# Row maxima of attention turned on VectorE instead of TensorE, and carried by four DMAs instead of two

## The chip, the cores and the metric

One core of one Trainium2 chip. The time is the device time of one execution in microseconds (us); lower is better.

## The reference

The input x has 8 batches of 1,024 tokens with 512 features. A layer of causal self-attention (16 heads of 32) with a residual and a layernorm is followed by a mixture-of-depths block: of each batch's 1,024 tokens, the 512 with the best router score go through a feed-forward net, and their result is added to the rows they came from.

```python
qkv = encodings @ W_attn + b_attn
scores = jnp.einsum('bhki,bhqi->bhkq', k, q) / math.sqrt(HEAD)
scores = jnp.where(mask, scores, jnp.float32(-10000.0))
attn = jax.nn.softmax(scores, axis=2)
combined = jnp.einsum('bhkq,bhkl->bhql', attn, v)
...
x = _layernorm(x + attn_out)
scores = jnp.einsum('bsd,d->bs', x, w_router)
top_scores, top_idx = jax.lax.top_k(scores, k)      # k = half of the tokens
h = gelu(selected @ W1 + b1);  processed = h @ W2 + b2
x = _layernorm(x + scatter(sigmoid(top_scores) * processed))
```

## The kernel before, in words

All five engines run hand-ordered streams that meet only through semaphores. A class `Table` lays the attention stage out in **beats**. A **unit** u (64 of them, `U = 8 * B`) is one batch, one group of four heads and one half of the queries (512). Two units, an even one (first half of the queries) and an odd one (second half), make a pair, and a pair takes 32 beats. Each engine's program walks over the beats n and issues in each what the table puts there, so the position in the table is only an order within each engine, not a time.

Per unit there are two passes over the scores. **Pass A** forms the scores with queries on the partitions, piece by piece (`a_piece` on TensorE, 11 pieces for an even unit, 27 for an odd one), into a ring of three PSUM banks (`A_BANKS`). VectorE takes the negated row maximum of each piece (`max_piece`) and collects them in `nm`: 128 queries by 16 numbers (4 heads by 4 blocks of 128 queries). **Pass B** (`b_tile`) forms the scores again with keys on the partitions. Its matmul has 98 rows in place of 96: rows 96 and 97 of `Qp` hold the negated maximum as a high and a low part, and the same rows of `Kp` hold ones, so that the maximum is subtracted inside the matmul. ScalarE then only takes the exponential (line 943). GpSimd masks and adds up (lines 795 and 818), and TensorE multiplies with V (line 1456) and forms the sums.

Pass A of an even unit lies at beats 0 to 8.5 of its pair, that of the odd unit at 8.5 to 30 (`A_AT`). Pass B lies at 28 to 36.5 and 36.5 to 58 (`B_AT`), so it runs into the next pair.

Between the two passes the 128 x 16 maxima must be turned to 16 x 128. In the kernel before this is an entry "F" of the ring at beat 15.99 or 31.99 (`F_AT`): `transpose_maxima` is one TensorE transpose (line 1411) into a ring bank. `shift_out` on VectorE copies it to `shs` as the high part (line 1061) and subtracts for the low part (line 1063). SyncE's queue then sends one DMA of 16 rows by 512 bytes for each part to rows 96 and 97 of `Qp` (line 670). The first B tile of the unit waits for both.

SyncE issues nearly every DMA of the kernel in the order of the table: loads of x and of the split weights, the stores and reloads of the attention output (`o_s`, `Ot`), and the packs of Q and K (`Qp<-nat`, `Kp<-nat`, line 687, three DMAs each). The attention stage also carries the "dense" work (projections, output projection O with its residual and layernorm statistics, sums N), cut into pieces and spread over the beats. After attention comes the feed-forward stage (lines 1491 and 1512), matmuls back to back.

Of the kernel before, what the change touches and what calls it, by code (L numbers as in the profile page):

```python
# [5 lines left out]
F32 = mybir.dt.float32  # L6
# [7 lines left out]
P = 128  # L14
# [19 lines left out]
BEATS = 16  # L34
A_AT = ((0.0, 8.5), (8.5, 30.0))
B_AT = ((28.0, 36.5), (36.5, 58.0))
F_AT = (15.99, 31.99)
A_BANKS = (0, 1, 2)
B_BANKS = (3, 4)
LAST_B = (4, 3, 0)  # L40
# [134 lines left out]
class Table:  # L175
# [68 lines left out]

    def streams(self):

        self.tiles, self.formed, self.products = {}, {}, {}
        ring = []
        for u in range(U):
            at, end = A_AT[u % 2]  # L250
            some = chunks(u)
            work = [1.3 if len(x[0]) == 4 else 0.8 if x[3] == 384 else 1.0 for x in some]
            for j, x in enumerate(some):
                p = u // 2 * 2 * BEATS + at + (end - at) * sum(work[:j]) / sum(work)
                ring.append((p, ("A", u, j, x)))
            ring.append((u // 2 * 2 * BEATS + F_AT[u % 2], ("F", u)))
            at, end = B_AT[u % 2]
            some = [(k, hh) for k in range(ksteps(u)) for hh in tiles_of(u, k)]
            work = [168 + 0.87 * width(u, k) * len(hh) for k, hh in some]
            for t, (k, hh) in enumerate(some):  # L260
                p = u // 2 * 2 * BEATS + at + (end - at) * sum(work[:t]) / sum(work)
                self.tiles.setdefault(int(p), []).append((p, (u, k, hh)))
                self.formed[u, k] = int(p + (end - at) * work[t] / sum(work) * (1 - 1 / len(hh)))
            for k in range(ksteps(u)):
                j, k1 = [(j, max(g)) for j, g in enumerate(PRODUCTS[u % 2]) if k in g][0]
                n = self.formed[u, k1] + PV_LAG[u % 2][j]
                assert not by_products(u) or n < self.beat["N", u]
                self.products.setdefault(n, []).append((u, k))
        self.scored = {}
        for b in range(B):  # L270
            self.scored[b] = self.beat["O", b, TT - 1] + 9 if b < B - 2 else self.beat["S", b]
            if b < B - 2:
                ring.append((self.scored[b] + 0.9, ("S", b)))
        self.ring, self.ring_no = {}, {}
        for j, (p, x) in enumerate(sorted(ring, key=lambda y: y[0])):
            self.ring.setdefault(int(p), []).append((p, j, x))
            self.ring_no[x[:3]] = j
# [85 lines left out]
def layer(nc, s, args, dr, cs, out):  # L363
    T = Table()
    x, xt, wqkv, wo, bat, b_out, w_router, W1, b1, W2, b2 = args
    with ExitStack() as st:
# [79 lines left out]
        maskA = sb("maskA", [P, 512], BF16)  # L446
        one32 = ones[:, 0:HD].bitcast(F32)
        nm = sb("nm", [P, 2, 2, HG, 4], F32)
        shs = sb("shs", [16, 2, P], F32R)
        lst_, lmv, lrs, lnb = sb("lnst", [P, 2, 6], F32), sb("lnmv", [P, 2, 2], F32), sb("lnrs", [P, 2, 2], F32), sb(  # L450
            "lnnb", [P, 2, 2], F32)
        li = sb("li", [P, 2, 4, 2], U32)
# [128 lines left out]
        def sync(e):  # L581
# [49 lines left out]
            for n in range(T.first, T.last):  # L631
# [29 lines left out]
                if n - 7 in load_v and 2 <= load_v[n - 7] < V_NEW:  # L661
                    q = load_v[n - 7]
                    e.wait_ge(s["v_split"], q + 1)
                    store(4 + q % 2, Wvf, s["v_st"])
                for a, x_ in T.ring_in(n - 1):
                    if x_[0] == "F":
                        u = x_[1]
                        e.wait_ge(s["a_max"], a + 1)
                        for j in range(2):
                            e.dma_start(Qp[96 + j:97 + j, u % 4, :, :].rearrange("a h (t n) -> a (h t) n", n=P)  # L670
                                        .bitcast(F32), shs[:, j, :].bitcast(F32)).then_inc(s["shift"], 16)
                for job in T.packs.get(n, ()):
                    e.wait_ge(*freed(job))
                    if job[0] == "Q":
# [351 lines left out]
        def vector(e):  # L1026
# [8 lines left out]

            def max_piece(j, u, i, piece):
                hh, qt, k0, w, part = piece
                if i == 0 and u >= 2:
                    e.wait_ge(s["a_mm"], T.ring_no["F", u - 2] + 1)
                e.wait_ge(s["a_mm"], j + 1)  # L1040
                if k0 < 512 * (u % 2):
                    ins = e.tensor_reduce(out=nm[:, u % 2, 0, hh[0], qt:qt + 1], in_=PS[:, A_BANKS[j % 3], :], op=ALU.max,  # L1042
# [9 lines left out]
                                                     accum_out=nm[:, u % 2, u % 2, h_, qt:qt + 1])  # L1052
                ins.then_inc(s["a_max"], 1)

            def shift_out(j, u):

                src = PS[0:16, A_BANKS[j % 3], 0:P]
                e.wait_ge(s["a_mm"], j + 1)
                if u:
                    e.wait_ge(s["shift"], 32 * u)  # L1060
                link(e.tensor_copy(shs[:, 0, :], src))
                linked()
                e.tensor_tensor(shs[:, 1, :], src, shs[:, 0, :].bitcast(F32), ALU.subtract).then_inc(s["a_max"], 1)

            def scores_out(j, b):
                e.wait_ge(s["a_mm"], j + 1)
# [2 lines left out]
                e.tensor_copy(sct[:, :], PS[0:TT, A_BANKS[j % 3], 0:P]).then_inc(s["a_max"], 1)  # L1069

            def ring_entry(j, x_):
                if x_[0] == "F":
                    shift_out(j, x_[1])
                elif x_[0] == "S":
                    scores_out(j, x_[1])
                else:
                    max_piece(j, *x_[1:])
# [149 lines left out]
            for n in range(T.first, T.last):  # L1227
# [9 lines left out]
                    ring_entry(*x_)  # L1237
                for job in todo:
                    evacuate(job)
                for x_ in some[1:]:  # L1240
                    ring_entry(*x_)
                for j in o_conv.get(n - 1, ()):
                    o = o_number(j)
                    t = j[2]
                    e.wait_ge(s["os_hi"], o + 1)
                    e.tensor_tensor(Os[:, 1, :, :], Ot[:, :, :], Os[:, 0, :, :].bitcast(F32),
                                    ALU.subtract).then_inc(s["os"], 1)
# [13 lines left out]
                if n in rank_beat:  # L1261
                    t = rank_beat[n]
                    if t == 0:
                        e.wait_ge(s["srow"], 16)
                    if t < TT:
                        count_ranks(e, s, cs, sc[:, 0, :], srow0, cmpb0, t)
                    else:
                        list_ranks(e, s, cs, 0)
                for k in range(KT):
                    if n - 6 - k in load_x:  # L1270
                        split_x(*load_x[n - 6 - k], k)
# [25 lines left out]
        def tensor(e):  # L1297
# [107 lines left out]
                                   start=True, stop=True)  # L1405
                ins.then_inc(s["a_mm"], 1)

            def transpose_maxima(j, u):
                e.wait_ge(s["a_max"], T.ring_no["A", u, len(chunks(u)) - 1] + 1)
                e.wait_ge(s["a_max"], j - 2)  # L1410
                e.transpose(PS[0:16, A_BANKS[j % 3], 0:P], nm[:, u % 2, u % 2, :, :].rearrange("p h t -> p (h t)"),
                            cs["identf"][:]).then_inc(s["a_mm"], 1)

            def transpose_scores(j, b):
                e.wait_ge(s["score"], TT * (b + 1))
                e.wait_ge(s["a_max"], j - 2)
                e.transpose(PS[0:TT, A_BANKS[j % 3], 0:P], sc[:, b, :], cs["identf"][:]).then_inc(s["a_mm"], 1)

            def ring_entry(j, x_):
                if x_[0] == "F":  # L1420
                    transpose_maxima(j, x_[1])
                elif x_[0] == "S":
                    transpose_scores(j, x_[1])
                else:
                    a_piece(j, *x_[1:])
# [1 line left out]
            def b_tile(u, k, hh):  # L1427
# [1 line left out]
                j = tiles_before(u, k) + tiles_of(u, k).index(hh)  # L1429
                w = width(u, k)  # L1430
                if k == 0 and hh[0] == 0:
                    e.wait_ge(s["shift"], 32 * (u + 1))
                if j == tiles_before(U - 1) + 2:
                    e.wait_ge(s["a_max"], len(T.ring_no))
                elif j >= 2:
# [123 lines left out]
        with nc.Block() as block:  # L1559
# [6 lines left out]

SEMAPHORES = ("c0", "bias", "b_scaled", "wq_in", "w1_in", "x0_hi", "rk0", "w_in", "w_hi", "w_split", "w_st", "v_in", "v_hi", "v_split", "v_st", "wo_in",
              "wo_hi", "wo_lo", "x_hi", "x_lo", "ones", "rows", "d_mm", "ev_v", "ev_a", "kq_hi", "a_mm", "a_max",
              "shift", "b_mm", "b_exp", "keep", "padd", "pv", "o_cp", "nln", "rinv", "ot", "os_hi", "os",
              "lmva", "rs", "hset", "oset", "score", "sge", "sig", "scd", "srow", "srow7", "rank_list", "v_link", "v_rank", "p_link",  # L1570
              "wlo2", "whi2", "fc", "f0", "f1", "f3", "fmv", "fst", "frs", "f_link", "p_sum", "ht", "t_hi", "hthi", "htlo", "up", "gelu",
              "ghi", "glo", "dn")
# [59 lines left out]
```

## Time and profile before

| what | value |
|---|---|
| time, median of 3 runs | 2560.07 us (2559.65 to 2562.88) |
| profiled execution: span from first to last instruction | 2558.8 us |
| TensorE busy | 2481.7 us, 97% of the span |
| VectorE / ScalarE / GpSimd busy | 65% / 47% / 61% |
| mean granted TensorE clock | 0.981 |

The page gives no device time of its own for the profiled execution; the median of the runs is 1.3 us above its span. Busy time of TensorE is modelled from pipelined matmuls: a matmul's duration is longer than the distance from its start to the next one's start, so the distance between starts is what it costs.

### The profile page before, as it was taken

How to read it: one execution, taken by the hardware profiler on the slowest of the kernel's cores; microseconds unless marked ns; L12 is line 12 of the kernel's file. 1: busy time of each engine (PE TensorE's matmuls, PEld its weight loads, DVE VectorE, ACT ScalarE, POOL GpSimd, SP SyncE). 2: the span in 40 equal slices, each digit the busy share in tenths (PEclk: the TensorE clock that was granted, in tenths of full speed). 3: DMA queues.
4: the chain of work that ended last, by engine and by line, in shares of the span. 5: the costliest groups of instructions: out<-in, count | busy, mean ns of one | idle time of the engine just before them, and what ended most of it. 6: DMA issues, size and time to landing. Idle time of an engine off the chain costs nothing.

```text
span 2558.8 us, 40698 instructions
## 1 busy us (share of the span) xinstructions
PE 2481.7 (97%) x14168; PEld 1834.9 (72%) x14168; DVE 1665.5 (65%) x4231; ACT 1190.7 (47%) x2034; POOL 1556.9 (61%) x1635
## 2 busy tenths in 40 slices
PE   7999999999999999999999999997999999999998
PEld 5666676777776777777776767773688888888886
DVE  6667677777776867877677777777555545553533
ACT  2555566656655655656656556565531111111110
POOL 1677788778887878888778877877232113121211
PEclk8999999999999999999999999998999999999999
DMA  7666677776577866767766676763420101010000
GB/s 146 90 108 139 126 144 172 140 150 157 129 144 130 193 128 127 175 127 153 151 145 146 125 167 137 155 154 97 152 91 25 34 25 42 25 34 25 22 29 17
DMA packets 167262, 286.46 MB, mean 112 GB/s; under 512 B 23121, under 2 KB 58001, under 8 KB 165906
## 3 DMA queue, kind: packets, MB, share of 16 engines
q1 hardware_dynamic: 159890, 267.01, 49.1%
q0 software_dynamic: 7168, 16.85, 2.1%
q8 instruction: 114, 1.87, 0.4%
q14 instruction: 90, 0.74, 0.1%
HBM read 116.97 MB, written 65.11 MB: 71 GB/s over the span
## 4 chain that ended last, share of the span: by engine, by line
PE 81%; POOL 2%; ACT 2%; DVE 1%; issue 1%; DMA 1%; SPq 1%; POOLq 0%; ACTq 0%; DVEq 0%
PE PS L1512 13%; PE PS L1491 13%; PE PS L1352 11%; PE PS L1438 10%; PE PS L1404 9%; PE PS L1456 8%; PE PS L1366 7%; PE PS L1360 6%; PE PS L1375 2%; POOL Pa L818 1%; PE PS L1368 1%; PE PS L1472 0%; PE PS L1333 0%; DMA h_s<-hs 0%; ACT Pm L943 0%
## 5 line engine op out<-in xcount | busy, mean ns | idle before, releaser
L818 POOL TENSOR_TENSOR Pa<-Pa,Pm 128x512 f32<-128x512 f32 (+1 forms) x602 | 743.8, 1259 | 114.4 <-ACT Pm L943 101.5
L1438 PE MATMUL PS<-Qp,Kp 98*128 98x512 f32 (+3 forms) x1536 | 494.9, 358 | 24.1 <-ACT Pm L943 13.2
L1404 PE MATMUL PS<-Kp,Qp 96*128 96x512 f32 (+3 forms) x1536 | 495.0, 359 | 17.4 <-DVE nm L1042 5.7
L943 ACT ACTIVATE Pm<-PS 128x512 f32<-128x512 f32 (+1 forms) x643 | 358.1, 568 | 282.6 <-PE PS L1438 243.5
L1042 DVE TENSOR_REDUCE nm<-PS 128x1 f32<-128x512 f32 x512 | 344.9, 687 | 183.7 <-PE PS L1404 183.6
L818 POOL TENSOR_TENSOR Pa<-Pa,P 128x512 f32<-128x512 f32 (+1 forms) x297 | 369.6, 1268 | 57.1 <-ACT P L943 50.1
L1404 PEld LDWEIGHTS PS<-Kp,Qp 96*128 96x128 f32 x1536 | 282.9, 193 | 118.5 <-issue 44.3
L1438 PEld LDWEIGHTS PS<-Qp,Kp 98*128 98x128 f32 x1536 | 281.7, 192 | 104.1 <-ACT Pm L943 27.4
L1050 DVE CUSTOM_DVE_ANT_0 PS<-PS,maskA 128x384 f32<-128x384 f32 (+3 forms) x512 | 245.9, 509 | 153.3 <-PE PS L1404 152.2
L908 ACT ACTIVATE G<-PS,b1c 128x512 f32<-128x512 f32 x128 | 88.2, 689 | 539.6 <-PE PS L1491 539.5
L1050 DVE CUSTOM_DVE_ANT_0 PS<-PS,maskA,nm 128x384 f32<-128x384 f32 (+3 forms) x512 | 267.0, 554 | 91.6 <-PE PS L1404 85.9
L1512 PE MATMUL PS<-W2h,Gs 128*128 128x512 f32 x1024 | 316.7, 390 | 0.9 <-DVE W2l L1144 0.9
L1491 PE MATMUL PS<-hT,W1h 128*128 128x512 f32 x1024 | 271.9, 389 | 0.0
L1195 DVE CAST Gs<-G 128x512 fp32r<-128x512 f32 x128 | 54.6, 427 | 306.9 <-ACT G L908 246.5
L943 ACT ACTIVATE P<-PS 128x512 f32<-128x512 f32 (+1 forms) x317 | 176.5, 569 | 132.8 <-PE PS L1438 115.1
L1491 PEld LDWEIGHTS PS<-hT,W1h 128*128 128x128 f32 x1024 | 192.1, 188 | 40.3 <-issue 0.2
L1512 PEld LDWEIGHTS PS<-W2h,Gs 128*128 128x128 f32 x1024 | 191.1, 188 | 40.0 <-issue 1.3
L943 ACT ACTIVATE Pa<-PS 128x512 f32<-128x512 f32 x256 | 149.1, 598 | 124.8 <-PE PS L1438 124.6
L1512 PE MATMUL PS<-W2l,Gs 128*128 128x512 f32 x512 | 199.2, 389 | 0.0
L783 POOL TENSOR_SCALAR rs<-mv 128x1 f32<-128x1 f32 x32 | 9.6, 301 | 304.8 <-DVE mv L1179 302.9
L1352 PE MATMUL PS<-xTh,Wkh 128*128 128x512 f32 x512 | 183.9, 412 | 8.8 <-ACT xTh L919 6.9
L1352 PE MATMUL PS<-xTh,Wkl 128*128 128x512 f32 x512 | 182.8, 411 | 0.0
(142 smaller groups left out, 4236.4 us busy)
## 6 DMA issues: line engine op xcount, KB each, us to landing
Qp<-nat SPq DMA_DIRECT2D x192, 256.0 KB, 7.4
Kp<-nat SPq DMA_DIRECT2D x192, 256.0 KB, 6.2
o_s<-Of SPq DMA_DIRECT2D x64, 256.0 KB, 2.3
Ot<-o_s SPq DMA_DIRECT2D x64, 256.0 KB, 3.1
xb<-in_x SPq DMA_DIRECT2D x64, 256.0 KB, 3.2
h_s<-hs SPq DMA_DIRECT2D x64, 256.0 KB, 2.3
out<-xb SPq DMA_DIRECT2D x64, 256.0 KB, 2.5
x_raw<-in_xt SPq DMA_DIRECT2D x15, 1024.0 KB, 6.4
```

What stands on the lines that cost most here:

```text
L818: e.tensor_tensor(to, to, probs(u, k)[:, h0:h0 + many, 0:w], ALU.add).then_inc(s["padd"], many)
L943: e.activation(probs(u, k)[:, hh[0]:hh[-1] + 1, 0:w], tile_bank(j)[:, 0:len(hh) * w].rearrange("p (h n) -> p h n", n=w), ACT.Exp).then_inc ...
L1042: ins = e.tensor_reduce(out=nm[:, u % 2, 0, hh[0], qt:qt + 1], in_=PS[:, A_BANKS[j % 3], :], op=ALU.max, axis=AX, negate=True)
L1050: ins = e.tensor_tensor_reduce(out=to, in0=to, in1=maskA[:, 512 - w:512], scale=-1.0, scalar=least, op0=ALU.add, op1=ALU.min, accum_out=nm ...
L1352: ins = e.matmul(to, Wk[wh][:, 1 if kind == "K" else 0, kt, :], xT[xh][:, kt, c * 512:c * 512 + 512], start=k == 0, stop=k == 11)
L1360: ins = e.matmul(to[:, t * 256:t * 256 + 256], xT[xh][:, kt, tok:tok + P], Wv[wh][:, kt, :], start=m == 0, stop=m == 11)
L1366: ins = e.matmul(to, Os[:, oh, kt, :], Wo[wh][:, kt, :], start=k == 0, stop=False)
L1404: ins = e.matmul(to, Qp[0:96, u % 4, h_, qt * P:qt * P + P], Kp[0:96, (2 * i + k0 // 512) % 4, h_, 0:w], start=True, stop=True)
L1438: ins = e.matmul(tile_bank(j)[:, x_ * w:x_ * w + w], Kp[0:98, (2 * i + k // 4) % 4, h_, k % 4 * P:k % 4 * P + P], Qp[0:98, u % 4, h_, 512 ...
L1456: ins = e.matmul(PO[32 * h_:32 * h_ + 32, 512 - w:512], V[:, (u // 4 * 4 + k // 2) % 6, k % 2, vo:vo + HD], probs(u, k)[:, h_, 0:w], start ...
L1491: ins = e.matmul(PS[:, UP_BANKS[j % 2], :], W1p[wh][k][:, f * P:f * P + P], hT[:, xh, k, :], start=n_ == 0, stop=n_ == 11)
L1512: ins = e.matmul(PS[:, DOWN_BANK + t, :], Gs[:, j % 3, gh, t * P:t * P + P], W2p[wh][f // 4][:, f % 4, :], start=f == 0 and n_ == 0, stop= ...
```

## The change

The entry F leaves the ring, and with it the TensorE transpose, its bank and the read from PSUM. In its place VectorE does three operations per unit, all from SBUF to SBUF, in the beat of the unit's last A piece and the one after it: it rounds the 16 maxima of each query into columns 0 to 15 of `split` (the high part), subtracts into columns 16 to 31 (the low part), and transposes the 128 x 32 array with its own 32 x 32 block transpose into `shs`. Block c of the result (partitions 32c to 32c+31) holds for each part, head and query block 32 neighbouring queries. Four DMAs, one for each c, 32 pieces of 128 bytes each, take them to rows 96 and 97 of `Qp`.

`self.shifts` is filled with `int(p)` after the loop over the pieces of A, so its beat is that of the unit's last A piece: beat 7 of the pair for an even unit and 29 for an odd one (before: 15 and 31). VectorE rounds in beat n, subtracts and turns in n+1, and SyncE issues in n+2.

```diff
-            ring.append((u // 2 * 2 * BEATS + F_AT[u % 2], ("F", u)))
+            self.shifts.setdefault(int(p), []).append(u)
...
-        shs = sb("shs", [16, 2, P], F32R)
+        split = sb("split", [P, 2, HG * 4], F32R)
+        shs = sb("shs", [P, HD], F32)
...
-                for a, x_ in T.ring_in(n - 1):
-                    if x_[0] == "F":
-                        u = x_[1]
-                        e.wait_ge(s["a_max"], a + 1)
-                        for j in range(2):
-                            e.dma_start(Qp[96 + j:97 + j, u % 4, :, :].rearrange("a h (t n) -> a (h t) n", n=P)
-                                        .bitcast(F32), shs[:, j, :].bitcast(F32)).then_inc(s["shift"], 16)
+                for u in T.shifts.get(n - 2, ()):
+                    e.wait_ge(s["turned"], u + 1)
+                    rows = Qp[96:98, u % 4, :, :].bitcast(F32).rearrange("j h (t b n) -> j b (h t) n", b=4, n=HD)
+                    for c in range(4):
+                        e.dma_start(rows[:, c, :, :], shs[32 * c:32 * c + 32, :]).then_inc(s["shift"], 16)
...
-                if i == 0 and u >= 2:
-                    e.wait_ge(s["a_mm"], T.ring_no["F", u - 2] + 1)
...
+            def shift_high(u):
+                e.wait_ge(s["a_max"], T.ring_no["A", u, len(chunks(u)) - 1] + 1)
+                e.tensor_copy(split[:, 0, :], maxima(u)).then_inc(s["sh_hi"], 1)
+
+            def shift_low(u):
+                e.wait_ge(s["sh_hi"], u + 1)
+                e.tensor_tensor(split[:, 1, :], maxima(u), split[:, 0, :].bitcast(F32),
+                                ALU.subtract).then_inc(s["sh_lo"], 1)
+
+            def shift_turn(u):
+                e.wait_ge(s["sh_lo"], u + 1)
                 if u:
-                    e.wait_ge(s["shift"], 32 * u)
-                link(e.tensor_copy(shs[:, 0, :], src))
-                linked()
-                e.tensor_tensor(shs[:, 1, :], src, shs[:, 0, :].bitcast(F32), ALU.subtract).then_inc(s["a_max"], 1)
+                    e.wait_ge(s["shift"], 64 * u)
+                e.transpose(shs[:, :], split[:, :, :].rearrange("p j m -> p (j m)").bitcast(F32)).then_inc(s["turned"], 1)
...
+                for u in T.shifts.get(n - 1, ()):
+                    shift_low(u)
                 for x_ in some[1:]:
                     ring_entry(*x_)
+                for u in T.shifts.get(n, ()):
+                    shift_high(u)
...
+                for u in T.shifts.get(n - 1, ()):
+                    shift_turn(u)
...
-            def transpose_maxima(j, u):
-                e.wait_ge(s["a_max"], T.ring_no["A", u, len(chunks(u)) - 1] + 1)
-                e.wait_ge(s["a_max"], j - 2)
-                e.transpose(PS[0:16, A_BANKS[j % 3], 0:P], nm[:, u % 2, u % 2, :, :].rearrange("p h t -> p (h t)"),
-                            cs["identf"][:]).then_inc(s["a_mm"], 1)
...
-                    e.wait_ge(s["shift"], 32 * (u + 1))
+                    e.wait_ge(s["shift"], 64 * (u + 1))
```

## Rows read from the trace of the kernel before

**Rows 1.** The page: busy time, and the chain that ended last.

```profile
PE 2481.7 (97%) x14168; PEld 1834.9 (72%) x14168; DVE 1665.5 (65%) x4231; ACT 1190.7 (47%) x2034; POOL 1556.9 (61%) x1635
...
PE 81%; POOL 2%; ACT 2%; DVE 1%; issue 1%; DMA 1%; SPq 1%; POOLq 0%; ACTq 0%; DVEq 0%
```

**Rows 2.** Waits of TensorE by releaser: total us, times, longest.

```profile
PE PS L1438 <- ACT Pm L943: 13.2, 8, 2.5
...
PE PS L1456 <- POOL Pm L795: 5.8, 3, 2.5
PE PS L1404 <- DVE nm L1042: 5.7, 5, 2.0
```

**Rows 3.** Windows: busy us (instructions) per engine, TensorE's granted clock, DMA share, GB/s.

```profile
646.97:650.38 3.41, 3.41 (x12) 3.02 (x11) 3.41 (x9) 0.99 (x3) 3.33 (x4) 0.50 0.06 22
863.00:866.40 3.40, 3.12 (x16) 2.74 (x17) 3.40 (x5) 2.42 (x6) 3.40 (x4) 1.00 0.11 42
70.00:1700.00 1630.00, 1602.20 (x10094) 1138.01 (x10096) 1180.70 (x3088) 975.12 (x1704) 1305.84 (x1328) 0.99 0.69 141
```

**Rows 4.** The tile nm: the transpose, durations as min/median/max ns.

```profile
L1411 PE MATMUL PS<-identf,nm x64: 272/274/415, 46.2 to 1760.4; 128*16 128x128 f32 x64
```

**Rows 5.** Timeline of TensorE around F of unit 20: start, duration, engine, line.

```profile
582.01 0.42 PE L1438 MATMUL PS<-Qp,Kp 98*128 98x512 f32 x1
582.27 0.27 PE L1411 MATMUL PS<-identf,nm 128*16 128x128 f32 x1
582.48 1.07 PE L1375 MATMUL PS<-Pa,ones 128*32 128x512 f32 x8
```

**Rows 6.** Timeline around F of unit 21 (odd), to its first B tile.

```profile
607.19 0.76 DVE L1050 CUSTOM_DVE_ANT_0 PS<-PS,maskA,nm 128x512 f32<-128x512 f32 x1 [1.92 <-PE PS L1404]
...
609.30 0.27 PE L1411 MATMUL PS<-identf,nm 128*16 128x128 f32 x1
609.31 0.69 DVE L1122 BATCH_NORM_STATS2 lnst<-xb 128x6 f32<-128x512 f32 x1
...
610.21 0.28 DVE L1063 TENSOR_TENSOR shs<-PS,shs 16x128 fp32r<-16x128 f32 x1
...
610.52 1.21 SPq L670 DMA_DIRECT2D Qp<-shs  x2
...
617.93 0.39 PE L1438 MATMUL PS<-Qp,Kp 98*128 98x512 f32 x1
```

**Rows 7.** The tile shs: what VectorE and SyncE do with it.

```profile
L670 SPq DMA_DIRECT2D Qp<-shs x128: 513/589/1535, 47.8 to 1762.6; - x128
L1061 DVE CAST shs<-PS x64: 261/269/280, 47.2 to 1761.4; 16x128 fp32r<-16x128 f32 x64
L1063 DVE TENSOR_TENSOR shs<-PS,shs x64: 278/279/279, 47.5 to 1761.7; 16x128 fp32r<-16x128 f32 x64
```

**Rows 8.** Groups of VectorE by line and form: busy us, mean ns, idle before.

```profile
L338 DVE COPY lst<-sg 128x8 f32<-128x8 f32 x8 | 1.3, 165 | 0.0
```

**Rows 9.** DMA issues: count, KB each, median us to landing.

```profile
Qp<-nat SPq DMA_DIRECT2D x192, 256.0 KB, 7.4
...
Qp<-shs SPq DMA_DIRECT2D x128, 8.0 KB
...
li<-list_s SPq DMA_DIRECT2D x8, 4.0 KB, 1.9
```

**Rows 10.** Timeline around a wait of TensorE for ScalarE, unit 22.

```profile
635.76 0.27 PE L1411 MATMUL PS<-identf,nm 128*16 128x128 f32 x1
...
636.13 5.00 POOL L818 TENSOR_TENSOR Pa<-Pa,P 128x512 f32<-128x512 f32 x4
...
642.56 0.27 POOL L834 TENSOR_SCALAR lnnb<-lnrs,lnmv 128x2 f32<-128x2 f32 x1
...
642.86 0.81 ACT L998 ACTIVATE hs<-xb,lnnb,lnrs 128x512 f32<-128x512 f32 x1 [0.92 <-POOL lnnb L834]
...
645.86 0.50 PE L1438 MATMUL PS<-Qp,Kp 98*128 98x512 f32 x1 [1.78 <-ACT Pm L943]
```

More of the change, by code:

```diff
@@ L36 @@
 B_AT = ((28.0, 36.5), (36.5, 58.0))
-F_AT = (15.99, 31.99)
 A_BANKS = (0, 1, 2)
@@ L245, in streams @@
     def streams(self):
-        self.tiles, self.formed, self.products = {}, {}, {}
+        self.tiles, self.formed, self.products, self.shifts = {}, {}, {}, {}
         ring = []
@@ L1053, in max_piece, with maxima @@
                 ins.then_inc(s["a_max"], 1)
-            def shift_out(j, u):
-                src = PS[0:16, A_BANKS[j % 3], 0:P]
-                e.wait_ge(s["a_mm"], j + 1)
+            def maxima(u):
+                return nm[:, u % 2, u % 2, :, :].rearrange("p h t -> p (h t)")
+            def shift_high(u):
[7 more added lines that the diff above has]
+                e.wait_ge(s["sh_lo"], u + 1)
                 if u:
-                    e.wait_ge(s["shift"], 32 * u)
-                link(e.tensor_copy(shs[:, 0, :], src))
-                linked()
-                e.tensor_tensor(shs[:, 1, :], src, shs[:, 0, :].bitcast(F32), ALU.subtract).then_inc(s["a_max"], 1)
+                    e.wait_ge(s["shift"], 64 * u)
+                e.transpose(shs[:, :], split[:, :, :].rearrange("p j m -> p (j m)").bitcast(F32)).then_inc(s["turned"], 1)
             def scores_out(j, b):
@@ L1071, in ring_entry @@
             def ring_entry(j, x_):
-                if x_[0] == "F":
-                    shift_out(j, x_[1])
-                elif x_[0] == "S":
+                if x_[0] == "S":
                     scores_out(j, x_[1])
@@ L1419, in ring_entry @@
             def ring_entry(j, x_):
-                if x_[0] == "F":
-                    transpose_maxima(j, x_[1])
-                elif x_[0] == "S":
+                if x_[0] == "S":
                     transpose_scores(j, x_[1])
@@ L1568 @@
               "wo_hi", "wo_lo", "x_hi", "x_lo", "ones", "rows", "d_mm", "ev_v", "ev_a", "kq_hi", "a_mm", "a_max",
-              "shift", "b_mm", "b_exp", "keep", "padd", "pv", "o_cp", "nln", "rinv", "ot", "os_hi", "os",
+              "sh_hi", "sh_lo", "turned", "shift", "b_mm", "b_exp", "keep", "padd", "pv", "o_cp", "nln", "rinv", "ot", "os_hi", "os",
               "lmva", "rs", "hset", "oset", "score", "sge", "sig", "scd", "srow", "srow7", "rank_list", "v_link", "v_rank", "p_link",
```

## The prediction

> **What bounds the kernel now.** I read the page first. TensorE is busy for 97% of the span, and the chain that ended last lies on it for 81%, with 2% at most on any other engine [rows 1]. Then the windows: from 70 us to 1700 us, where the attention stage runs, it is busy 1602.2 of 1630 us at a mean granted clock of 0.99, while VectorE has 449 us to spare and GpSimd 324 us [rows 3]. The last view is the waits of TensorE by releaser. The largest for ScalarE, GpSimd and VectorE are 13.2, 5.8 and 5.7 us, in 16 waits together [rows 2]. So TensorE bounds the kernel. An edit is worth what it takes off TensorE's stream, plus or minus what it does to those few waits. The feed-forward stage is not touched.
>
> **TensorE: 64 transposes go.** One transpose lasts 274 ns in the median [rows 4], but the engine is pipelined, so I take distances between starts. Around unit 20, the transpose starts at 582.27 and the next matmul at 582.48: 0.21 us [rows 5]. The matmul ahead of it starts at 582.01. That distance of 0.26 us is about what a matmul of 512 columns takes anyway, so at most some 0.02 us belong to the change of weights. The transposes of units 10 to 63 all show 0.20 or 0.21. The removed work is 64 x 0.21 = 13.4 us, and with the 0.02 it would be 14.7. The lower bound of one removal is 0, where another engine holds the next matmul.
>
> **What of it is given back.** In each batch there is one place where TensorE waits 1.78 us for an exponential of ScalarE (1.0 in the first batch). I count seven in the timeline, from 319.7 to 1518.7 us, and show the one of unit 22. ScalarE is late there because two evictions of the layernorm wait for GpSimd (line 834, ending at 642.83), and GpSimd had been adding since 636.13 [rows 10]. F of unit 22 ran at 635.76, just ahead of these adds, when ScalarE was already evicting the first tile they take. So the chain does not shorten with it: GpSimd is the limit from F to the end of the wait. So TensorE arrives 0.2 us earlier and waits 0.2 us longer, at 7 of 64. I also count units 0 and 1 (the pipeline is filling, with waits for DMA and weights) and 62 and 63 (the drain, with ScalarE and VectorE in the chain) as given back. Together 11 x 0.21 = 2.3 us. The waits for GpSimd's masking, 5.8 us in 3 times [rows 2], and one short wait more near 232 us could take 4 more, 0.8 us, which I keep for the range.
>
> **The ring.** Without F, the ring holds 38 pieces a pair in place of 40. A piece waits for the maximum of the piece three before it. The five waits for `nm` of line 1042 sum to 5.7 us in the whole run [rows 2], and those of line 1050 to about the same, nearly all in the filling and in the drain. A ring with two entries fewer gives 0 in the steady stretch; I bound its gain by 1 us for the ends.
>
> **VectorE.** Removed are a copy of 269 ns and a subtraction of 279 ns a unit [rows 7], 35 us in all. Added are a copy and a subtraction over 128 x 16 and the block transpose over 128 x 32. The trace has a copy over 128 x 8 at 165 ns [rows 8]; I take 0.17 us each for the first two. It has no block transpose. From below it is that 165 ns copy, since 32 columns aren't fewer than 8. From above I take a 128-column pass at 279 ns. I choose 0.2 us, nearer the copy, as 32 columns are nearer to 8 than to 128. So 0.54 us are added for 0.55 removed, and between 0.50 and 0.62 the balance is within 5 us of VectorE's time, which lies in its 449 us to spare: 0 on the path. If that cover were gone, the cost would be the balance, 4 us at most. The Trainium skill (VectorE: DVE Perf Modes, The three transpose paths) gives 311 ns for a VectorE transpose of 128 x 128 and says it is made of separate 32 x 32 blocks. With 311 for my 0.2 the balance would be 7 us over all 64 units, still inside that spare time; no run shows it yet.
>
> **Waits on VectorE.** The three operations wait only for VectorE's own earlier results, where before it waited for TensorE's transpose. Nothing of another engine can hold them. `shift_turn` also waits for the DMAs of the unit before, over 10 us old.
>
> **SyncE's queue.** One issue takes 0.589 us [rows 7]. Two a unit are added, 1.2 us. What is queued behind them in an odd unit is the reload `Ot`, then xb, in one unit of four a block of x, the store of `Of` and the stores of the layernorm. Their order after the shift stays the same. In an even unit the shift now comes at beat 9 of the pair, after the pack of K at beat 5 and ahead of loads of weights and x at beats 10 to 12. It is done some 2.4 us after VectorE's beat 8, before those loads are due. `Ot` and xb no longer stand behind the shift there, and may start earlier. I cost this at 0. Its cover is that the consumers are beats away: `Ot` is converted six beats after its issue. A beat is (609.30 - 582.27)/16 = 1.69 us [rows 5, 6], so that is 10 us.
>
> **Does pass B get its rows in time?** This is the step that could turn the sign, and it is tight only in odd units. For unit 21, the last maximum starts at 607.19 and is done at 607.95. VectorE's next work is the residual add and the statistics of O, done at 610.00 [rows 6]. The rounding fits ahead of them, and the subtraction and the turn end at about 610.00 + 0.17 + 0.2 = 610.4. That is the moment at which the old kernel was ready too (610.21 + 0.28 = 610.49). Four issues start at 610.4 and the last ends at 612.8, having started at 612.2. The landing of 8 KB has no row. The nearest of that size is 4 KB in 1.9 us, and the farthest a 256 KB pack at 7.4 us [rows 9]. I take 1.9, the nearest in size: 614.1. The first B tile starts at 617.93 [rows 6], so 3.6 us are left after its weights. In an even unit, the turn is near beat 8 and pass B at beat 28, 20 beats or 34 us later, so nothing can go wrong. Costs 0; at 7.4 us landing it would be 612.2 + 7.4 - 617.7 = 1.9 us an odd unit.
>
> The Trainium skill (DMA: Bandwidth & Descriptors, Specifications) says that pieces under 512 bytes do not run at line rate, and the change goes from 512 to 128 bytes. The same page (Why small descriptors are slow) confines the penalty to HBM and exempts SBUF to SBUF, which is the case here. By the first rule the landing moves toward the late end above, by the second it stays; no row before shows 128-byte pieces.
>
> **The sum.** 13.4 - 2.3 = 11.1 us off the span of 2558.8: 2547.7. The median stands 1.3 us above the span, so 2560.07 - 11.1 = **2549.0 us**.
>
> **The clock.** The window from 646.97 has a granted clock of 0.50 (1.2 GHz) right after TensorE's wait of 1.78 us; after the same wait in the batch of 863 the clock stays at 1.00 [rows 3, 10]. So such a wait costs either nothing more or about half of 3.4 us, 1.7 us. The change shifts each of the seven waits in time. Of the seven, four were followed by the lower clock, and one or two more or fewer is chance: plus or minus 3.4 us. The Trainium skill (TensorE: Matmul & The Clock Gate, What's actually happening) has the same two levels and says that the point of change varies with phase; the rows above agree with both.
>
> **The rivals.**
> - *The gain is given back in full or mostly.* The stream of units could be paced by GpSimd (1305.8 of 1630 us busy [rows 3]) or by ScalarE, with TensorE's 0.2 us a unit becoming wait. For it: the seven places. Against it: 1602 us busy and pieces spaced without idle time in every pair between them. Time: 2556 to 2561, from 64 x 0.21 with three quarters or more given back.
> - *Slower: pass B waits for the four DMAs in odd units.* Place: the wait for `shift` at the first B tile. It starts when the last DMA lands more than 5.5 us after its issue, and decides the sign from 32 x wait > 11.1 us, a landing over 5.9 us. Price at the 7.4 us row: 32 x 1.9 = 61 us, so 2549 + 61 = 2610. At 6.2 us it would be 2549 + 32 x 0.7 = 2571. For it: the packs of Q and K take that long [rows 9], and smaller pieces are four times as many. Against it: those are three transfers of 256 KB queued together, these are 4 KB each with an empty queue behind them.
> - *A larger gain.* Fewer of the seven waits are followed by the lower clock, or the bookkeeping ahead of GpSimd's part (the aggregation, which VectorE now reaches half a microsecond earlier in even units) shortens the waits by up to 0.5 us each. Time: 2549 - 3.4 - 3.5 = 2542 at the end, 2545 in the middle.
> - *The transpose's time was free.* If TensorE's stream had hidden it, nothing would come. The starts in [rows 5] speak against it.
>
> **How the numbers follow.** Measurement of this kernel can tell 0.2%, 5.1 us, from no change. My forecast, 2546.5 to 2553, gets 0.66, the larger gain 0.14, the gain mostly given back 0.13, and pass B waiting 0.07. The range of 2543.5 to 2555.5 takes in the forecast, the larger gain but its tail, and the edge of the given-back case, and leaves out some 2 in 10. Faster by over 0.2% (below 2555): 0.66 + 0.14 + 0.03 of the given-back case = 0.83. Within: 0.10 of that case and 0.01 of the waiting one, 0.11. Slower: 0.06.
>
> **What the profile after would show.** Line 1411 gone; TensorE's busy time lower by 13 to 18 us, as overlaps with its neighbours are counted or not (64 x 274 ns is 17.5). Two successive F-free units of a steady pair shorter by 0.42 us. VectorE's busy time within 5 us. Four issues a unit on SyncE, still near 0.59 us. No wait for a DMA at line 1438. The wait of TensorE for ScalarE once a batch still there, longer by some 0.2 us. Wrong would be: a wait for `Qp<-shs` at the B tile of odd units, issues of over 1 us each, a block transpose of over 1 us, or more places with a clock of 0.50.

## The result, and the profile after

The changed kernel takes 2573.71 us in the median (2571.49 to 2575.93, 4 runs) against 2560.01 us (4 runs): a ratio of 1.0043, 95% interval 1.003 to 1.0055. It is 13.7 us slower, where 11.1 us faster was forecast. The profiled execution has a span of 2574.2 us, 15.4 us above that of before.

The page of the changed kernel, busy time and the chain by engine:

```profile
PE 2483.6 (96%) x14104; PEld 1836.4 (71%) x14104; DVE 1665.6 (65%) x4295; ACT 1191.2 (46%) x2034; POOL 1556.3 (60%) x1635
...
PE 38%; POOL 3%; ACT 1%; DVE 1%; issue 1%; DMA 0%; SPq 0%; POOLq 0%; ACTq 0%; DVEq 0%
```

The transposes are gone (14104 matmuls for 14168), and yet TensorE's modelled busy time didn't fall [rows 1]: 2483.6 for 2481.7. The shares of the chain can't be compared with those of before. The profile follows this chain back from the end only to 1434 us (44% of the span in all), and that of before to 277 us; the 38% don't say that TensorE bounds the kernel less. The waits of TensorE after, total us, times and longest:

```profile
PE PS L1438 <- ACT Pm L941: 17.2, 8, 2.8
PE PS L1412 <- DVE nm L1046: 12.2, 11, 2.1
PE PS L1438 <- ACT P L941: 9.0, 5, 2.8
...
PE PS L1412 <- DMA Kp<-nat: 3.1, 1, 3.1
```

The rows of before that [rows 2] doesn't have:

```profile
PE PS L1438 <- ACT P L943: 7.0, 5, 2.2
...
PE PS L1404 <- DVE nm L1050: 5.2, 5, 2.1
PE PS L1404 <- DMA Kp<-nat: 4.8, 2, 3.1
```

The two ScalarE rows went from 13.2 + 7.0 to 17.2 + 9.0, 6.0 us more in as many waits: 1.78 us once a batch became 2.79. The wait for the maxima of line 1050 (now 1046) went from 5.2 to 12.2 us and from 5 to 11 waits. Six stand once a batch, 6.4 us together, where before there was one of 0.63 us; one more, of 1.17 us, lies in the drain. No row has line 1438 waiting for a DMA, so pass B had no wait for its maxima that the list would show (it lists those above 0.15 us). VectorE's three operations by tile:

```profile
L1056 DVE CAST split<-nm x64: 151/175/616, 42.3 to 1774.8; 128x16 fp32r<-128x16 f32 x64
L1060 DVE TENSOR_TENSOR split<-nm,split x64: 155/164/552, 43.0 to 1775.0; 128x16 fp32r<-128x16 f32 x64
L1067 DVE STREAM_TRANSPOSE shs<-split x64: 201/211/214, 43.2 to 1776.3; 128x32 f32<-128x32 f32 x64
```

They sum to 0.55 us in the medians, where 0.54 was forecast.

### The profile page after: what moved, and what is told of

The parts are those of the page before. It is cut to its first block and busy times, and to the rows that moved or that the text cites. A ratio compares the mean times of both kernels' runs of the same rounds, so it can differ in the third digit from the quotient of the medians.

```text
span 2574.2 us, 40636 instructions
## 1 busy us (share of the span) xinstructions
PE 2483.6 (96%) x14104; PEld 1836.4 (71%) x14104; DVE 1665.6 (65%) x4295; ACT 1191.2 (46%) x2034; POOL 1556.3 (60%) x1635
## 5 line engine op out<-in xcount | busy, mean ns | idle before, releaser
L1438 PE MATMUL PS<-Qp,Kp 98*128 98x512 f32 (+3 forms) x1536 | 495.6, 359 | 31.3 <-ACT Pm L941 17.2
L1412 PE MATMUL PS<-Kp,Qp 96*128 96x512 f32 (+3 forms) x1536 | 496.4, 360 | 23.7 <-DVE nm L1046 12.2
```

The costliest lines, as they stand in the source:

```text
L1412: ins = e.matmul(to, Qp[0:96, u % 4, h_, qt * P:qt * P + P], Kp[0:96, (2 * i + k0 // 512) % 4, h_, 0:w], start=True, stop=True)
L1438: ins = e.matmul(tile_bank(j)[:, x_ * w:x_ * w + w], Kp[0:98, (2 * i + k // 4) % 4, h_, k % 4 * P:k % 4 * P + P], Qp[0:98, u % 4, h_, 512 ...
```

## Where the time went, in four places

**TensorE around the transpose.** Unit 20 of the changed kernel:

```profile
586.40 0.41 PE L1438 MATMUL PS<-Qp,Kp 98*128 98x512 f32 x1
...
586.74 1.06 PE L1383 MATMUL PS<-Pa,ones 128*32 128x512 f32 x8
```

Before, the matmul ahead of F and the one behind it were 0.47 us apart [rows 5]. Now they are 0.34 apart, where the prediction's working needs 0.26. In the medians of units 10 to 63, 0.12 us are saved in even units and 0.11 in odd ones, not 0.21. The next matmul (32 columns of weights) starts 0.34 us behind this one, where the ordinary ones just ahead start 0.23 apart. The transpose had stood in part in that longer distance. What makes it longer, the type or the narrow weights, no run separates.

**The even units give it back.** Unit 26, with the timing of the old kernel first, then of the new, in a batch stretch without any listed wait:

```profile
752.40 0.82 ACT L998 ACTIVATE hs<-xb,lnnb,lnrs 128x512 f32<-128x512 f32 x1 [0.30 <-POOL lnnb L834]
...
754.11 0.40 PE L1404 MATMUL PS<-Kp,Qp 96*128 96x512 f32 x1
...
754.46 0.50 PE L1438 MATMUL PS<-Qp,Kp 98*128 98x512 f32 x1
```

```profile
758.16 0.82 ACT L996 ACTIVATE hs<-xb,lnnb,lnrs 128x512 f32<-128x512 f32 x1 [0.42 <-POOL lnnb L832]
...
759.75 0.40 PE L1412 MATMUL PS<-Kp,Qp 96*128 96x512 f32 x1
...
760.22 0.50 PE L1438 MATMUL PS<-Qp,Kp 98*128 98x512 f32 x1
```

ScalarE's eviction (line 998, now 996) waited 0.30 us for GpSimd and now waits 0.42. The B tile at the end started 0.35 us behind the matmul ahead of it and now starts 0.47 behind: the 0.12 us gained at F is gone 8 us later. The starts of pass B in successive units show it all along. Away from the places with longer waits, the new kernel gains 0.09 to 0.14 us with each odd unit and 0.00 with each even one (within 0.02). What stays of 13.4 us is 32 x 0.11 = 3.5.

**SyncE's queue, once a batch.** Unit 29 after, and the same stretch before:

```profile
833.46 2.65 SPq L669 DMA_DIRECT2D Qp<-shs  x4
...
837.80 0.59 SPq L604 DMA_DIRECT2D x_raw<-in_xt  x1
...
839.10 0.43 SPq L699 DMA_DIRECT2D h_s<-hs  x1
...
848.01 0.69 DVE L1264 CUSTOM_DVE_ANT_0 hs<-hs,wrB 128x512 f32<-128x512 f32 x1 [4.61 <-DMA h_s<-hs]
...
849.52 0.56 PE L1412 MATMUL PS<-Kp,Qp 96*128 96x512 f32 x1 [1.46 <-DVE nm L1046]
```

```profile
827.95 1.21 SPq L670 DMA_DIRECT2D Qp<-shs  x2
...
830.56 1.09 SPq L604 DMA_DIRECT2D x_raw<-in_xt  x1
...
832.69 0.43 SPq L701 DMA_DIRECT2D h_s<-hs  x1
...
839.88 1.02 DVE L1258 CUSTOM_DVE_ANT_0 hs<-hs,wrB 128x512 f32<-128x512 f32 x1 [2.04 <-DMA h_s<-hs]
```

Four issues take 2.65 us, two took 1.21, and SyncE has no pause here until it has worked off what piled up. The load of 1 MB of x was issued 2.13 us ahead of the 256 KB store of the hidden rows and now stands 1.30 us ahead of it. VectorE gets past the store 8.9 us after its issue and no longer 7.2. Measured from where VectorE comes to line 1264, the store is also issued 0.85 us later, so VectorE waits 4.61 us and no longer 2.04. Its maxima stand behind that in the same stream, and TensorE waits 1.46 us for a ring bank. There are six such waits, of 0.66 to 1.65 us.

The closer distance alone doesn't explain the longer landing. In the changed kernel it is 1.30 us in all six batches, and the store lands 7.2 to 9.4 us after its issue. Before, it was 1.3 to 2.1 us, and the store landed after 6.3 to 9.3. VectorE's wait for it was 1.1 to 4.9 us before (2.4 in the mean of the six) and is 2.8 to 4.8 after (3.9). What all of them share is that the load stands ahead of the store.

**A race of VectorE and GpSimd, once a batch.** Unit 30, after and before:

```profile
867.90 0.68 DVE L1141 TENSOR_TENSOR xTl<-x_raw,xTh 128x512 fp32r<-128x512 f32 x1
867.97 1.18 POOL L829 TENSOR_TENSOR lnrs<-lnrs,half 128x2 f32<-128x2 f32 x1
...
869.10 0.68 DVE L1141 TENSOR_TENSOR xTl<-x_raw,xTh 128x512 fp32r<-128x512 f32 x1
869.25 0.66 POOL L832 TENSOR_SCALAR lnnb<-lnrs,lnmv 128x2 f32<-128x2 f32 x1
...
872.95 0.50 PE L1438 MATMUL PS<-Qp,Kp 98*128 98x512 f32 x1 [2.79 <-ACT P L941]
```

```profile
859.16 0.71 POOL L831 TENSOR_TENSOR lnrs<-lnrs,half 128x2 f32<-128x2 f32 x1
...
859.23 0.68 DVE L1139 TENSOR_TENSOR xTl<-x_raw,xTh 128x512 fp32r<-128x512 f32 x1
...
859.98 0.27 POOL L834 TENSOR_SCALAR lnnb<-lnrs,lnmv 128x2 f32<-128x2 f32 x1
...
863.28 0.50 PE L1438 MATMUL PS<-Qp,Kp 98*128 98x512 f32 x1 [1.78 <-ACT P L943]
```

Before, GpSimd's power operation started 0.07 us ahead of VectorE's subtraction (both operands in SBUF) and took 0.71 us. After, it starts 0.07 us behind it and takes 1.18, and the scaling behind it, 0.15 us behind the next subtraction, takes 0.66 for 0.27. The same holds in all six batches, and wherever else this order occurs. Of the runs below, x_late in both its executions, act_two and old_act have it. In these and the changed kernel, the power operation starts 0.06 to 0.23 us behind the start of the subtraction in 29 batches, and each time it ends 1.25 us behind that start, however early it began itself. By these times it waits until the subtraction of 0.68 us is over.

Together with the 0.12 us by which TensorE now arrives early, ScalarE's eviction, the rounding of x and the exponential come 1.0 us later, in each of the six batches. The Trainium skill (SBUF — State Buffer, Terms) says that VectorE and GpSimd arbitrate for one pair of SBUF ports, held for a full instruction, and that the loser blocks. The durations above agree with that, but for one that is told with new_dve; no run here shows the port itself.

The granted clock changes too. Behind the new wait at 849.5 us and behind that at 873 us:

```profile
849.70:853.10 3.40, 3.40 (x14) 1.38 (x13) 3.12 (x10) 1.54 (x2) 0.00 (x0) 0.51 0.88 133
873.60:877.00 3.40, 3.40 (x12) 2.90 (x11) 2.63 (x4) 1.34 (x3) 3.32 (x4) 0.51 0.00 0
```

Both are at half rate (1.2 GHz); before, the wait of that batch had no such stretch behind it [rows 3]. Between 400 and 1700 us there are eight such stretches, where before there were five. The mean granted clock fell from 0.981 to 0.979, which over the span is about 5 us. A part of this can be chance, as the length of a wait doesn't decide whether a stretch follows: of the six waits for ScalarE once a batch, four had one behind them before (1.78 us each), six in the changed kernel (2.79), and four and five in two executions of x_late (2.79 too).

The account for the profiled executions: -3.5 (kept), +6.0 (ScalarE), +7.0 - 0.5 (maxima, line 1050 and its wait at F), +0.6 (maxima, line 1042), -1.7 (a wait for a pack of K that went), +5 (clock) = 12.9 of 15.4 us. The rest lies in the first and the last units: pass B of unit 0 starts 1.3 us later and that of unit 63 loses 1.2. The first of these comes and goes with the execution: it is 0.0 in x_late and 1.3 in pad_even.

## The experiments

Each was timed beside the kernel before on the same chip; its medians there were 2561.5, 2561.9 and 2562.0 us in the three sets, and the ratios are against those. The changed kernel itself ran in another set, so it is compared with these runs by the ratios (its own is 1.0043, 1.003 to 1.0055).

**pad: give TensorE back what the transpose cost, and some more.**

```diff
+                        e.matmul(to[0:32, 0:P], one32, acc[:, u % 2, 0, 0:P], start=True, stop=True)
                         for h_ in range(4):
                             ins = e.matmul(to[32 * h_:32 * h_ + 32, :], one32, acc[:, u % 2, h_, :], start=True,
```

The added matmul's result is written over by the next one.

> The changed kernel with a dummy TensorE matmul of 128 fp32 columns ahead of the sums N of units 0 to 61, where the transpose stood; it writes columns that the next matmul overwrites. It gives TensorE back the cost of the transpose and nothing else. Theory 1, a race of VectorE and GpSimd: the yearly wait of TensorE for ScalarE once a batch grew from 1.78 to 2.79 us because, with TensorE 0.13 us ahead of GpSimd's adds, VectorE's subtraction now starts 0.07 us before GpSimd's power operation and not after it, and GpSimd's two operations take 1.18 and 0.66 us instead of 0.71 and 0.27. Then the wait goes back to about 1.78 in six batches, and the time is about the changed kernel's, 2569 to 2576, since 8 us of added work stand against 6 us and some clock. Theory 2, SyncE's queue alone: the wait stays 2.79, and the time goes up by about 8 us to 2582. Both expect the six new waits of 0.66 to 1.65 us for the maxima to stay.

2568.51 us (2562.32 to 2573.19, 6 runs), ratio 1.003 (1.0017 to 1.0043). That is 0.5 us below the expected range. By the ratios it is 3 us faster than the changed kernel, with 62 matmuls more, but the two intervals overlap. The dummy isn't the transpose's equal: from the last B tile ahead of the sums to the work behind them an even unit takes 0.21 us more than in the changed kernel, where the transpose cost 0.12, and an odd unit 0.19 more. The wait once a batch is 1.71 us in all six, and GpSimd's power operation is back at a mean of 712 ns (757 in the changed kernel, 711 before):

```profile
L829 POOL TENSOR_TENSOR lnrs<-lnrs,half 128x2 f32<-128x2 f32 x64 | 45.5, 712 | 5.3
```

VectorE's subtraction now starts 0.14 us behind GpSimd's power operation, so TensorE's timing alone turns the race round. The waits for the maxima vary: the profiled execution, the fastest at 2562.3 us, has only two of them (0.66 and 0.67 us) and one for a pack of K.

**x_late: the load of x behind the store.**

```diff
-                if n in load_x and load_x[n][0] > 0:
-                    x_half(*load_x[n])
...
                     e.dma_start(xb[:, o % 2, :], xr[j[1], j[2]]).then_inc(s["xb", o % 2], 16)
+                if n in load_x and load_x[n][0] > 0:
+                    x_half(*load_x[n])
```

> The changed kernel with SyncE issuing the load of the next batch's x after the store of the hidden rows of the same beat instead of ahead of it. Theory 2, the queue: the four issues end 1.4 us later than the two did, the load of 1 MB stands closer ahead of the store h_s, which lands after 8.9 us instead of 7.2, VectorE waits for it and TensorE for VectorE. Then the six waits of TensorE for the maxima at line 1046 between 400 and 1520 us, 6.4 us in all, go, with one or two of the stretches at half clock: 2562 to 2568. If those waits have another cause they stay, and the time is 2572 to 2576. The wait of 2.79 us for ScalarE once a batch stays by either theory.

2560.25 us (2558.37 to 2561.87, 10 runs), ratio 0.9996 (0.9987 to 1.0006). The time is 1.7 us below the expected range, and by the ratios two lines of order take back 12 us. All six waits are gone; the wait of 2.79 us is still there. The store, now issued 1 us ahead of the load, lands 3.1 to 4.4 us after its issue. Unit 29, with the store ahead of the load and VectorE without idle time at line 1264:

```profile
832.62 0.43 SPq L697 DMA_DIRECT2D h_s<-hs  x1
...
833.57 0.61 SPq L604 DMA_DIRECT2D x_raw<-in_xt  x1
...
837.65 0.14 DVE L1046 DVE_READ_ACCUMULATOR2_ANT nm<- 128x1 f32 x1
837.65 0.68 DVE L1264 CUSTOM_DVE_ANT_0 hs<-hs,wrB 128x512 f32<-128x512 f32 x1
```

**act_two: two of the four DMAs issued by ScalarE.**

```diff
-                    for c in range(4):
+                    for c in range(2):
...
+                for u in T.shifts.get(n - 2, ()):
+                    e.wait_ge(s["turned"], u + 1)
...
+                    for c in range(2, 4):
+                        e.dma_start(rows[:, c, :, :], shs[32 * c:32 * c + 32, :]).then_inc(s["shift"], 16)
```

The added lines stand in ScalarE's loop, ahead of the copy of the output.

> The changed kernel with two of the four DMAs issued by ScalarE in the same beat, so that SyncE issues two as before the change. Theory 2, SyncE's queue: the six waits for the maxima go back, 6 to 9 us less, unless ScalarE's issues cost it as much as they cost SyncE (0.63 us each, 80 us over the run on an engine that idles half of the time); 2564 to 2570. A rival: the bytes in small pieces are what delays the store, not the issues; then the waits stay and the time is 2572 to 2580.

2570.91 us (2568.68 to 2571.72, 5 runs), ratio 1.0039 (1.0024 to 1.0053): by the ratios no different from the changed kernel. Two waits for the maxima of 0.68 us are left and two for a pack of K (0.71 and 1.83). An issue costs ScalarE as much as SyncE, 0.62 us in the median, and TensorE now waits some 0.2 us for ScalarE in three of the four pairs of each batch. The expected range was missed by 1 us. The run separates little: two effects of the same edit may cancel, and that the small pieces delay the store isn't excluded by it.

**old_four: the old kernel with four issues.**

```diff
                         for j in range(2):
-                            e.dma_start(Qp[96 + j:97 + j, u % 4, :, :]..., shs[:, j, :]...)
+                            for r in range(2):
+                                e.dma_start(Qp[96 + j:97 + j, u % 4, 2 * r:2 * r + 2, :]..., shs[8 * r:8 * r + 8, j, :]...)
```

> The kernel before, transposes on TensorE kept, with each of its two DMAs cut in two (8 rows of 512 bytes each), so four issues a unit. Theory 2: the issues alone bring the new waits of TensorE for the maxima, once a batch, about 1 us each, with some clock: 2566 to 2572. Theory 1 alone would leave it at 2558 to 2562. The wait for ScalarE once a batch stays at 1.78 us by both, since TensorE's timing is not touched.

2569.27 us (2567.57 to 2573.78, 7 runs), ratio 1.003 (1.0019 to 1.0042): 7.8 us slower than before by the issues alone. The wait for ScalarE stays at 1.79. The new waits are three of 0.64 to 0.70 us for the maxima and three of 2.5 to 3.0 us for a pack of K, so the late transfer can be another one. Its pieces are still of 512 bytes, so small pieces aren't needed for the loss:

```profile
PE PS L1406 <- DMA Kp<-nat: 11.2, 4, 3.1
```

**new_dve: x_late, with VectorE's subtractions of x a beat later.**

```diff
-                    if n - 6 - k in load_x:
-                        split_x(*load_x[n - 6 - k], k)
+                    if n - 7 - k in load_x:
+                        split_x(*load_x[n - 7 - k], k)
```

> The changed kernel with the load of x behind the store (as x_late) and VectorE's subtractions that split the next batch's x one beat later. By the race theory, the wait of TensorE for ScalarE once a batch falls from 2.79 to 1.78 us or less, as GpSimd's power operation (1.19 us in x_late at this place) and scale (0.66) are back at 0.71 and 0.27: six times 1.0 us and up to two stretches at half clock less than x_late: 2550 to 2555. If the place of the subtractions has nothing to do with it, the wait stays at 2.79 and the time at x_late's 2560.

2571.86 us (2567.98 to 2572.8, 6 runs), ratio 1.0037 (1.0025 to 1.005). The power operation is at 712 ns again and the wait once a batch fell from 2.79 to 2.10 us, not to 1.78, since the scaling behind it took 0.80, though it is recorded as starting 0.06 us ahead of a subtraction. But the split of x is now late for the projection, with up to 2.3 us once a batch:

```profile
655.98 0.50 PE L1360 MATMUL PS<-xTh,Wkh 128*128 128x512 f32 x1 [2.29 <-DVE xTl L1141]
```

So the expected time was missed by 17 us: the edit shortens one wait and makes others.

**new_act and old_act: ScalarE's second rounding of x a beat later**, on top of x_late and on the old kernel.

```diff
-                if n - 6 in load_x:
-                    split_x(*load_x[n - 6], 1)
+                if n - 7 in load_x:
+                    split_x(*load_x[n - 7], 1)
```

> The changed kernel with the load of x behind the store, and ScalarE's second rounding of the next batch's x (1.04 us) one beat later, so that it no longer stands between the two layernorm evictions and the exponentials. The wait once a batch of 2.79 us is then shorter by the 1.04 us whatever its first cause, 1.7 us, and if the clock no longer falls behind it, three stretches less: 2549 to 2555. If ScalarE isn't what TensorE waits for there, no change from 2560.

2558.16 us (2554.25 to 2559.47, 10 runs), ratio 0.9984 (0.9974 to 0.9993). The expected range ended at 2555. The wait went from 2.79 to 1.84 us, but a stretch at half clock still lies behind four of the six, and 2 to 3 us came of it where 5 or more were expected. The edit also moves VectorE's subtraction, which needs ScalarE's rounding. The power operation is at 712 ns, but now the operation ahead of it, 0.19 us long in the changed kernel, starts 0.04 us behind a subtraction and takes 0.69:

```profile
856.47 0.68 DVE L1141 TENSOR_TENSOR xTl<-x_raw,xTh 128x512 fp32r<-128x512 f32 x1
856.51 0.69 POOL L826 TENSOR_SCALAR lnrs<-lnmv 128x1 f32<-128x1 f32 x1
...
857.29 0.71 POOL L829 TENSOR_TENSOR lnrs<-lnrs,half 128x2 f32<-128x2 f32 x1
```

> The kernel before with both edits of new_act. The wait once a batch of 1.78 us goes to under 1 us and three or four stretches at half clock with it: 2556 - 6 - 6 = 2545 to 2552. Against new_act it tells what the transposes are worth on TensorE once both side effects are out: by the trace of the changed kernel 0.13 us a unit, so this one would be 6 to 8 us slower than new_act; by the prediction's 0.21 us, 11 to 13 us slower.

2562.71 us (2557.48 to 2565.34, 10 runs), ratio 1.0003 (0.9994 to 1.0013). A clear miss. The wait is 1.84 us here too, longer than the 1.78 it had: the old kernel now loses the race. Its power operation, 711 ns on the mean before:

```profile
L831 POOL TENSOR_TENSOR lnrs<-lnrs,half 128x2 f32<-128x2 f32 x64 | 47.9, 748 | 5.3
```

In both of these kernels the queue is in order and GpSimd's four operations of the layernorm take long, 2.23 us in new_act and 2.38 here (1.60 before, 2.48 in the changed kernel), and the wait is the same. So they compare the transposes nearly fairly: new_act is 4.6 us faster, where 6 to 8 were expected from 0.13 us a unit. A part can be the clock, as the profiled execution of old_act has a stretch at half clock behind all six waits.

**old_late: the old kernel with the order of x_late**, run in two sets.

> The kernel before with the load of x behind the store. If the queue's bunching is a matter of the change alone, this brings little: it has one wait for the maxima of 0.63 us and one for a pack of K of 1.72 us with half clock behind it, so at most 4 us: 2556 to 2560.

> The kernel of old_late once more, on the same chip as pad_even: 2555 to 2559. The comparison with pad_even tells what the change is worth with both side effects out; by the odd units alone it is 3.5 us.

2556.88 us (10 runs), ratio 0.9982 (0.9971 to 0.9993), and 2557.84 us (11 runs), ratio 0.998 (0.9971 to 0.9989). The old kernel had a part of the same fault, worth 4 to 5 us. Both medians lie in the expected ranges.

**pad_even: x_late, with the dummy matmul in even units alone.**

```diff
+                        if u % 2 == 0:
+                            e.matmul(to[0:32, 0:P], one32, acc[:, u % 2, 0, 0:P], start=True, stop=True)
```

> The changed kernel with the load of x behind the store and the dummy matmul of 128 fp32 columns ahead of the sums N of even units alone. In even units the time that the transpose took on TensorE is given back within 8 us anyway, at the B tile that waits for ScalarE, so the dummy costs nothing there; but it puts VectorE back behind GpSimd at the place of the race once a batch. Then the wait for ScalarE once a batch is 1.7 to 1.8 us in place of 2.79, the odd units keep their 0.11 us each, 3.5 us in all, and the time is below x_late by about 6 us and below old_late by about 3.5: 2552 to 2556. If the race is not set by TensorE's timing, it is x_late's 2560; if the dummy isn't free, 2556 to 2560.

2552.34 us (2550.85 to 2552.94, 5 runs), ratio 0.9963 (0.995 to 0.9977), as expected. It is the fastest of all, 9.7 us below the kernel before and 5.5 below old_late5. GpSimd is first again, and the wait is 1.71 us in all six batches:

```profile
642.28 0.71 POOL L829 TENSOR_TENSOR lnrs<-lnrs,half 128x2 f32<-128x2 f32 x1
642.42 0.68 DVE L1141 TENSOR_TENSOR xTl<-x_raw,xTh 128x512 fp32r<-128x512 f32 x1
...
646.40 0.50 PE L1440 MATMUL PS<-Qp,Kp 98*128 98x512 f32 x1 [1.71 <-ACT Pm L941]
```

```profile
PE PS L1440 <- ACT Pm L941: 12.6, 8, 2.5
...
PE PS L1440 <- ACT P L941: 6.9, 5, 2.2
```

Beside it on that chip ran x_late again.

> The kernel of x_late once more, on the same chip as pad_even: 2559 to 2562, with the wait of 2.79 us once a batch.

2560.21 us (2558.01 to 2561.48, 11 runs), ratio 0.9995 (0.9986 to 1.0004). So 31 dummy matmuls make it 7.9 us faster: 6.4 us less in the two ScalarE rows (12.6 + 6.9 for 16.9 + 9.0), and the profiled execution has three stretches at half clock between 400 and 1700 us where that of x_late has five.

## Why the prediction was wrong, by its steps

- *"64 x 0.21 = 13.4 us" removed from TensorE.* Mis-sized. The distance from F to the next matmul isn't what F's removal gives: the distance ahead of the next matmul grows by 0.08. It is 0.12 in even units and 0.11 in odd ones, 7.5 us in all.
- *"Given back ... at 7 of 64."* Wrong in its count. It took the seven waits that the list shows. GpSimd and ScalarE also set the start of one B tile in every even unit, with a wait of 0.12 us that no list shows because it is only a wider distance between two starts. The 32 even units keep nothing. The rule used there for seven was right and held for 32.
- *"Waits 0.2 us longer."* Wrong: 1.0 us longer. The step took the durations of GpSimd's operations as fixed. They depend on who starts first, VectorE or GpSimd, 0.07 us apart. That was nowhere among the rivals. pad and pad_even show it, and the 29 batches in which the power operation ends 1.25 us behind the subtraction's start.
- *"SyncE's queue ... I cost this at 0."* The step that cost most. It asked whether the consumers of what is queued behind are beats away, for `Ot`, and didn't ask it for the store of the hidden rows. Its consumer is VectorE, three beats later, and it stands behind a load of 1 MB. In the batch shown, 1.4 us more of issue became a store issued 0.85 us later that took 1.7 us more to land; over the run it became six waits of TensorE. VectorE waited for that store already before. x_late shows what the order costs (12 us with clock), old_four that four issues do it without the rest of the change (7.8 us). Why the landing is later isn't shown beyond the order of load and store.
- *Pass B gets its rows in time.* Right: no wait. *VectorE 0 on the path, 0.54 us a unit.* The time is right, 0.55 measured, and the block transpose took 211 ns for the 0.2 chosen.
- *The clock, plus or minus 3.4 us.* The mechanism was right, the size too small: there were three more such stretches net between 400 and 1700 us, with two behind the new waits for the maxima, and about 5 us.
- *TensorE's busy time lower by 13 to 18 us, and two successive units shorter by 0.42.* Wrong: 1.9 us higher, and 0.12 shorter. The clock and the smaller saving account for a part of the first; the rest is open.
- *The waits of line 1042 lie nearly all in the filling and the drain.* Misread: 2.9 of their 5.7 us lie between 196 and 201 us. Nothing hangs on it.
- The rival of a gain mostly given back ended at 2561. By its time the slower rival was the nearest (2571 at a landing of 6.2 us), but that would have been luck: it had the four DMAs landing late, and what landed late were others.

With the queue in order and GpSimd ahead, the change is worth 5.5 us (pad_even against old_late5), half of the forecast. The odd units account for 3.5 of it. The dummies shorten the six waits from 1.80 to 1.71 us, which gives 0.5, and the profiled executions differ by one stretch at half clock, about 1.7. Left open: why the landing times, and with them the waits for the maxima or for the pack of K, differ between executions of one kernel by several us (pad, 2562.3 to 2573.2), and what sets the first unit's 1.3 us.

## What to carry to other kernels

Measure the price of an operation on a full engine between its two neighbours, before and with the operation thought away, not from its start to the next. Look for places where starts are wider apart than they need be: each of them eats a gain of a tenth of a microsecond, unseen in any list of waits. When issues are added to a queue, follow every transfer behind them to its consumer, above all a small one that stands behind a large one. A faster engine changes who comes first elsewhere, so after such a change look at the durations of operations that weren't touched.

## What was not expected of the hardware

A GpSimd operation on 128 x 2 elements takes 0.71 or 1.18 us, and one on 128 x 2 of another kind 0.27 or 0.66, as it starts 0.07 us ahead of or behind a 0.68 us subtraction of VectorE from SBUF. In new_act one on 128 x 1 takes 0.69 us for 0.19, 0.04 us behind. The power operation ends 1.25 us behind the subtraction's start in all 29 batches in which it is second, by 0.06 to 0.23 us. In new_dve the scaling took 0.80 us though it is recorded as starting 0.06 us ahead, while the power operation isn't slowed 0.05 us ahead (old_late), so the recorded starts alone don't decide it. VectorE's 32 x 32 block transpose of 128 x 32 fp32 elements takes 211 ns. A DMA issue costs 0.62 us on ScalarE as on SyncE. A 256 KB store issued 1.3 us behind a 1 MB load lands 7.2 to 9.4 us after its issue in the changed kernel, and 3.1 to 4.4 us after it when issued 1 us ahead of the load (x_late).
